# Two reordered stretches of products, one redistributed store tile, and later weight loads in a six-stage perceiver kernel

## The chip, the cores and the metric

The kernel runs on one core of one Trainium2 chip, as one program. The metric is the device time of one execution in microseconds (us), as the median of several runs. The engines are TensorE (PE; its weight loads are listed as PEld), VectorE (DVE), ScalarE (ACT), GpSimd (POOL) and SyncE (SP), which here issues nearly all DMAs.

## What is computed

The reference takes 512 tokens of 256 channels (16 sequences of 32) and a context of 16 x 512 x 256, and adds six sublayers one after the other, each on the layer-normed x:

```python
x = x + _L0_xattn_ref(_layernorm(x), ctx_2048, ...)        # X0: cross-attention, int8 fake-quantised
x = x + _L0_attn_ref(_layernorm(x), ...)                   # A0: differential attention, 16 heads
x = x + _L0_ffn_ref(_layernorm(x), ...)                    # F0: gated feed-forward, fp8 casts
x = x + _L1_xattn_ref(_layernorm(x), ctx_2048, mask, ...)  # X1: masked cross-attention
x = x + _L1_attn_ref(_layernorm(x), ...)                   # M1: latent attention with rope
x = x + _L1_ffn_ref(_layernorm(x), ...)                    # F1: h = square(relu(fp8 matmul)); fp8 matmul
```

In F1 both operands of both products are scaled by their largest absolute value and rounded to fp8 e4m3. For cross-attention the keys and values of all 16 context sequences are projected, and every head's scores run over 512 keys.

## The kernel before

The six stages (X0, A0, F0, X1, M1, F1) are written out as straight code for each engine; semaphores order the engines among each other, and every engine runs its instructions in the order in which they are written. A buffer region in SBUF, the "arena", is divided between the stages, so a weight load of a later stage can only be issued once the earlier owner of its place has finished.

**Units.** Both cross-attentions project context sequence `b` in four units (`unit_pe`, L390 for the keys and L398 for the values; 2 or 4 products each of 128x512 or 128x256; an fp32 product stands as two records in the trace, so these are groups of 4 and 8). Units of X1 already run inside A0 and F0, where PE would otherwise wait: in A0 units 0 to 7, in `attn.pe` (L1241 on).

**X1 by batches.** `batch_cols_pe(b)` runs, for b = 0 to 15: the scores of sequence b (L443, 32 records), the values of sequence b - 1 (`values`, L478: 64 products of 128x32 with 17 columns of weights, 128 records), then up to three units of a later sequence, mixed with the steps that close a row tile (L495, L512, L521). Each group of values raises `x1_pv`, four for a sequence, so `s_pv >= 4 * k` means that the values of the first k sequences are done. DVE clips the scores (L844), evicts some units (L696, L698), and in batches 6 to 13 rounds a piece of F1's weights (`weights_dve`, L1609 and L1402 to L1405).

**Loads beside X1.** SP loads the context of sequence b when unit 4(b - 2) is done (`load_later`), and around it the weights of F1 and M1. For M1 these are five loads for `w_down` and small tables (L1853), three for the rope part of the query weights (L1856, rows of 64 words), two of 768 KB for `wq_upT` (L1861, "heads"), two of 512 KB for `wkv_upT` (L1864, "up"), and two of 1 MB for `wo_rows` (L1868, "out"). PE's first use of the last nine is `fold(0)` (L1897), behind the scores of the last batch and waiting for all nine.

**End of A0.** After the last head's values come the output products of head 14 (`out_rows`, L1232, waiting for ScalarE's copy L1298), unit 3 of X1 (L398), and the transposes of head 15 (L1225).

**End of F1.** The rounded hidden activation is held as a part `high8` (fp8) and a part `low8` (bf16), eight slices h of 128 hidden channels each. 64 products (L1658) add high8[h] and low8[h] times the weights into two PSUM banks: `ACC[0]` for the row tiles t = 0 and 1, `ACC[1]` for t = 2 and 3. A slice's four products, one for each row tile, stand together; high8[h] comes before low8[h - 1]. The last product into a bank raises `s_rows`. Then DVE scales and adds the row tiles of `ORDER` = 0, 1, 3 (L1775), ScalarE scales tile 2 (L1703) and GpSimd adds it to x (L1619); SP stores three tiles (L1788), ScalarE's queue the fourth (L1783). DVE's tile 3 waits for ScalarE's read of the same bank (`s_kept` at 3).

Of the kernel before, what the change touches and what calls it, by code (L numbers as in the profile page):

```python
# [14 lines left out]
P = 128  # L15
NB = 16
SQ = 32
D = 256
NC = D // P
ROWS = NB * SQ  # L20
NT = ROWS // P
# [3 lines left out]
H = 16  # L25
# [72 lines left out]
X0, A0, F0, X1, M1, F1 = range(6)  # L98
# [952 lines left out]
def attn(nc, e, take, sem, d):  # L1051
# [23 lines left out]
    PROJ, TB, ACC = (B[0], B[1]), B[5], (B[6], B[7])  # L1075
# [61 lines left out]
    ORDER, LEAD = (4, 0, 1, 5, 2, 3), 5  # L1137
# [103 lines left out]
    def pe(pe):  # L1241
# [29 lines left out]
        values(pe, H - 1)  # L1271
        out_rows(pe, H - 2)
        for u in units(3):
            e.phases[X1].unit_pe(pe, u)
        turn(pe, H - 1)
        for u in units(4):
# [264 lines left out]
def ffn1(nc, e, take, sem, d):  # L1541
# [22 lines left out]
    BY_ACT, BY_DVE = (2, 4, 6), (0, 1, 3, 5, 7)  # L1564
    ORDER = (0, 1, 3)
    last = wide([P, D])
# [49 lines left out]
    def pool(g):  # L1616
        t = NT - 2
        g.wait_ge(s_kept, 3)
        nc.gpsimd.tensor_tensor(e.X[:, t, :], e.X[:, t, :], last, ALU.add).then_inc(s_last, 1)  # L1619
# [6 lines left out]
    def pe(pe):  # L1626
# [19 lines left out]
        keep_busy(nc, e, HB[1], 10)  # L1646
        for h in range(HT + 1):
            for part, i, first, final in ((high8, h, h == 0, False), (low8, h - 1, False, h == HT)):
                if not 0 <= i < HT:
                    continue  # L1650
                if part is high8:
                    pe.wait_ge(s_h8, 2 * h + 1)
                elif i in BY_ACT:
                    pe.wait_ge(s_relu, HT + BY_ACT.index(i) + 1)
                else:
                    pe.wait_ge(s_y8, 2 + BY_DVE.index(i) + 1)
                for t in range(NT):
                    ins = nc.tensor.matmul(ACC[t // 2][:, (t % 2) * D:(t % 2 + 1) * D], part[:, i, t * P:(t + 1) * P], wp8[:, i, :],  # L1658
                                           start=(first and t % 2 == 0), stop=(final and t % 2 == 1))
                    if final and t % 2:  # L1660
                        ins.then_inc(s_rows, 1)

# [7 lines left out]
    def act(act):  # L1670
# [25 lines left out]
        for h in range(HT):  # L1696
            nc.scalar.activation(z[h], hid[:, h, :], ACT.Square, scale=both[:, 2:3]).then_inc(s_z, 1)
            if h in (4, 6, 7):
                low_act(act, BY_ACT[(4, 6, 7).index(h)])
        t = NT - 2  # L1700
        act.wait_ge(s_rows, 2)
        act.wait_ge(s_scale, 4)
# [21 lines left out]
    def dve(v, done):  # L1724
# [47 lines left out]
        for t in ORDER:  # L1772
            v.wait_ge(s_rows, t // 2 + 1)
            v.wait_ge(s_kept, 3 if t == NT - 1 else 2)
            nc.vector.scalar_tensor_tensor(out=e.X[:, t, :], in0=ACC[t // 2][:, (t % 2) * D:(t % 2 + 1) * D],  # L1775
                                           scalar=both[:, 1:2], in1=e.X[:, t, :], op0=ALU.mult, op1=ALU.add)\
              .then_inc(s_final, 1)
        v.sem_inc(done, 1)

    def store_last(act, out):  # L1780
        t = NT - 2
        act.wait_ge(s_last, 1)
        act.dma_start(out[t * P:(t + 1) * P, :], e.X[:, t, :]).then_inc(e.s_done, 16)  # L1783
# [17 lines left out]
def mla(nc, e, take, sem, d):  # L1801
# [45 lines left out]
    def load(sp):  # L1847
        cols = lambda a: a.rearrange("(c p) n -> p c n", p=P)
        rope_of = lambda i: d.wq_rope_halves[P:QR, :].rearrange("p (j i w) -> p i j w", i=2, w=ROPE)[:, i]
        loads = [(wd, cols(d.w_down)), (scales, d.latent_scales), (cossin, d.rope_rows), (rope, d.rope_cols), (mask32, d.causal)]  # L1850
        assert len(loads) == N_W
        for dst, src in loads:
            sp.dma_start(dst, src, allow_slow_non_contiguous=True).then_inc(s_w, 16)  # L1853
        for dst, src in ((wq0[:, :, 1::2, :], d.wq_rope_halves[0:P, :].rearrange("p (j i w) -> p j i w", i=2, w=ROPE)),
                         (wq1[half(0), :, 1, :], rope_of(0)), (wq1[half(1), :, 1, :], rope_of(1))):
            sp.dma_start(dst, src).then_inc(s_head_in, 16)  # L1856
# [307 lines left out]
    def dve(v, done):  # L2164
# [24 lines left out]
        def residual(t):  # L2189
# [3 lines left out]

    return Named(load_heads=load_heads, load_up=load_up, load_out=load_out, load=load, pool=pool, pe=pe, act=act, dve=dve, during_x1_pe=during_x1_pe, during_x1_act=during_x1_act,
                 during_x1_dve=during_x1_dve, during_x1_pool=during_x1_pool)
# [9 lines left out]
def build(nc, d, out, stages=6):  # L2205
    with ExitStack() as ctx:
# [31 lines left out]
        def _(sp):  # L2238
# [21 lines left out]
            if ph(X1):  # L2260
# [4 lines left out]
                def beside_x1(b):  # L2265
# [4 lines left out]
                    if b == 13 and ph(M1):  # L2270
                        sp.wait_ge(done[F0], 1)
                        sp.wait_ge(phases[X1].s_pv, 4 * 7)
                        phases[M1].load(sp)
                        phases[M1].load_heads(sp, 0)
                    elif b == 14 and ph(M1):
                        phases[M1].load_heads(sp, 1)
                    elif b == 15 and ph(M1):
                        phases[M1].load_up(sp, 0)
                phases[X1].load_later(sp, 3, beside_x1)
                if ph(M1):  # L2280
                    sp.wait_ge(phases[X1].s_pv, 4 * 9)
                    phases[M1].load_up(sp, 1)
                    sp.wait_ge(phases[X1].s_pv, 4 * 10)
                    phases[M1].load_out(sp, 0)
                    sp.wait_ge(phases[X1].s_pv, 4 * 11)
                    phases[M1].load_out(sp, 1)
            if ph(F1):
# [120 lines left out]
```

## Time and profile before

| | us |
|---|---|
| median of 3 runs | 652.62 |
| the runs | 651.98, 652.62, 655.08 |
| the profiled execution | 651.91 |
| its span, first to last instruction | 650.1 |
| PE busy | 634.4 (98%) |
| DVE busy | 417.1 (64%) |
| ScalarE busy | 279.6 (43%) |
| share of PE in the chain that ended last | 89% |

The span is 1.8 us shorter than the time of the same execution. Times of the trace count from the first instruction. The page divides the span in 40 slices of 16.25 us; X1's batches lie between about 390 and 535 us, M1's pairs of heads between 555 and 619, F1 from 620 on. Idle time of an engine is given together with what ended it; "issue" means that nothing which the profile shows held it. Instructions of the engines come by DMA too, in a queue of their own for PE, listed as "instruction".

### The profile page before, as it was taken

How to read it: one execution, taken by the hardware profiler on the slowest of the kernel's cores; microseconds unless marked ns; L12 is line 12 of the kernel's file. 1: busy time of each engine (PE TensorE's matmuls, PEld its weight loads, DVE VectorE, ACT ScalarE, POOL GpSimd, SP SyncE). 2: the span in 40 equal slices, each digit the busy share in tenths (PEclk: the TensorE clock that was granted, in tenths of full speed). 3: DMA queues.
4: the chain of work that ended last, by engine and by line, in shares of the span. 5: the costliest groups of instructions: out<-in, count | busy, mean ns of one | idle time of the engine just before them, and what ended most of it. 6: DMA issues, size and time to landing. Idle time of an engine off the chain costs nothing.

```text
span 650.1 us, 21669 instructions
## 1 busy us (share of the span) xinstructions
PE 634.4 (98%) x9613; PEld 435.0 (67%) x9614; DVE 417.1 (64%) x972; ACT 279.6 (43%) x516; POOL 59.7 (9%) x131
## 2 busy tenths in 40 slices
PE   9999999999999999999999999999979999999997
PEld 5666666667676676666667666777657775456785
DVE  3755467686764665555663772655868965687677
ACT  3454444545353334333343844544435553111156
POOL 1020000000001111101111003000110101000000
PEclk9999999999999999999999999999989999999999
DMA  7242111116006411110013620212373000000001
GB/s 246 66 171 67 35 34 34 68 35 216 15 3 225 134 34 35 34 34 1 2 35 86 208 65 33 68 35 68 80 245 112 24 5 1 2 3 3 4 1 34
DMA packets 28957, 42.25 MB, mean 65 GB/s; under 512 B 6080, under 2 KB 18880, under 8 KB 28352
## 3 DMA queue, kind: packets, MB, share of 16 engines
q1 hardware_dynamic: 28432, 40.47, 19.1%
q8 instruction: 76, 1.25, 0.8%
q10 hardware_dynamic: 432, 0.39, 0.2%
q14 instruction: 17, 0.14, 0.1%
HBM read 40.33 MB, written 0.52 MB: 63 GB/s over the span
## 4 chain that ended last, share of the span: by engine, by line
PE 89%; DVE 8%; issue 2%; ACT 1%; POOLq 0%; DVEq 0%; POOL 0%; ACTq 0%
PE psum L398 17%; PE psum L390 16%; PE psum L1185 7%; PE psum L478 6%; PE psum L443 5%; PE psum L453 4%; PE psum L1161 4%; PE psum L1232 4%; PE psum L1985 2%; PE psum L428 2%; PE psum L1202 2%; PE psum L1962 2%; PE psum L1943 2%; PE psum L1216 1%; DVE arena L2092 1%
## 5 line engine op out<-in xcount | busy, mean ns | idle before, releaser
L398 PE MATMUL psum<-arena 128*128 128x256 f32 x512 | 121.4, 383 | 0.8 <-issue 0.8
L390 PE MATMUL psum<-arena 128*128 128x512 f32 x248 | 118.9, 606 | 0.0
L398 PEld LDWEIGHTS psum<-arena 128*128 128x128 f32 x512 | 94.0, 190 | 22.9 <-issue 10.5
L390 PEld LDWEIGHTS psum<-arena 128*128 128x128 f32 x248 | 44.2, 192 | 41.6 <-issue 40.3
L711 ACT ACTIVATE arena<-arena 128x512 f32<-128x512 f32 x64 | 48.3, 805 | 41.7 <-DVE arena L844 41.7
L1293 ACT ACTIVATE arena<-psum 128x512 f32<-128x512 f32 x48 | 28.4, 597 | 66.2 <-PE psum L1185 37.6
L1185 PE MATMUL psum<-y_cols,arena 128*128 128x512 f32 x112 | 52.1, 599 | 0.0
L705 ACT ACTIVATE arena<-psum,arena 128x512 f32<-128x512 f32 x64 | 40.2, 688 | 27.0 <-DVE arena L831 26.9
L831 DVE TENSOR_REDUCE arena<-psum 128x1 f32<-128x512 f32 x64 | 39.7, 682 | 16.0 <-PE psum L428 15.8
L478 PEld LDWEIGHTS psum<-arena 128*17 128x17 f32 x4096 | 38.6, 96 | 16.0 <-issue 13.6
L685 ACT ACTIVATE arena<-psum,arena 128x512 f32<-128x512 f32 x43 | 29.5, 686 | 45.8 <-PE psum L390 41.1
L844 DVE TENSOR_SCALAR arena<-psum 128x512 f32<-128x512 f32 x64 | 39.7, 681 | 11.8 <-PE psum L443 10.8
L478 PE MATMUL psum<-arena 128*17 128x32 f32 x4096 | 43.1, 197 | 4.0 <-issue 3.9
L687 ACT ACTIVATE arena<-psum 128x512 f32<-128x512 f32 x41 | 24.5, 598 | 47.6 <-PE psum L398 47.5
L1347 DVE TENSOR_REDUCE arena<-psum 128x8 f32<-128x256 f32 x16 | 6.8, 424 | 51.1 <-PE psum L1202 51.1
L443 PEld LDWEIGHTS psum<-arena 64*128 64x128 f32 x512 | 29.8, 188 | 8.0 <-issue 8.0
L328 POOL TENSOR_TENSOR arena<-arena,head_mask 128x64 f32<-128x64 f32 (+1 forms) x64 | 20.7, 348 | 141.7 <-PE psum L428 87.3
L836 DVE COPY arena<-psum 128x512 f32<-128x512 f32 x32 | 22.0, 691 | 17.0 <-PE psum L453 16.5
L443 PE MATMUL psum<-arena 64*128 64x128 f32 x512 | 32.9, 278 | 0.0
L1185 PEld LDWEIGHTS psum<-y_cols,arena 128*128 128x128 f32 x112 | 20.6, 190 | 18.1 <-issue 17.2
L453 PEld LDWEIGHTS psum<-ident,arena 128*128 128x128 f32 x256 | 28.8, 141 | 4.5 <-issue 3.7
L1161 PE MATMUL psum<-arena,y_cols 128*128 128x256 f32 x128 | 31.1, 385 | 0.0
(260 smaller groups left out, 952.6 us busy)
## 6 DMA issues: line engine op xcount, KB each, us to landing
arena<-in_ctxT SPq DMA_DIRECT2D x31, 512.0 KB, 3.7
arena<-in_L_attn_Wv SPq DMA_DIRECT2D x1, 2048.0 KB, 8.1
arena<-in_L_attn_Wq SPq DMA_DIRECT2D x8, 256.0 KB, 2.9
arena<-in_L_attn_Wk SPq DMA_DIRECT2D x8, 256.0 KB, 3.6
arena<-in_L_attn_Wo SPq DMA_DIRECT2D x1, 2048.0 KB, 11.6
arena<-in_L_ffn_w_gating SPq DMA_DIRECT2D x1, 2048.0 KB, 7.8
arena<-in_wo_rows SPq DMA_DIRECT2D x2, 1024.0 KB, 4.9
arena<-in_wq_upT SPq DMA_DIRECT2D x2, 768.0 KB, 7.1
```

What stands on the lines that cost most here:

```text
L390: last = nc.tensor.matmul(bank, wkv[:, c, i * P:(i + 1) * P], x[:, c, :], start=(c == 0), stop=(c == NC - 1))
L398: last = nc.tensor.matmul(bank[:, kk * D:(kk + 1) * D], x[:, c, k * P:(k + 1) * P], wkv[:, c, D:2 * D], start=(c == 0), stop=(c == NC - 1))
L443: ins = nc.tensor.matmul(S[2 * kp + r][:, (2 * kk + h) * P:(2 * kk + h + 1) * P], kT[home(b)][a, h, k * P:(k + 1) * P], qbd[b % QBUFS][a, ...
L453: last = nc.tensor.transpose(S[g][:, k * P:(k + 1) * P], pr[g][:, k * P:(k + 1) * P], e.ident)
L478: last = nc.tensor.matmul(O[b % 2][j * SQ:j * SQ + VW, g * SQ:(g + 1) * SQ], va[home(b)][:, k, head, :], probs[:, j * SQ:(j + 1) * SQ], st ...
L685: ins = nc.scalar.activation(kT[home(b)][:, i, :], U[i % 2], ACT.Identity, bias=bk[:, i:i + 1])
L705: nc.scalar.activation(pr[g], S[g], ACT.Exp, bias=nmx[:, g:g + 1]).then_inc(s_exp, 1)
L711: nc.scalar.activation(pTk[b % 2][k], clip[k // 2][:, k % 2, :], ACT.Exp, bias=mb[:, b, k:k + 1], scale=m01[:, b, k:k + 1]).then_inc(s_exp, 1)
L831: nc.vector.tensor_reduce(nmx[:, g:g + 1], S[g], AX.X, ALU.max, negate=True).then_inc(s_mx, 1)
L844: nc.vector.tensor_scalar(dst, S[i].rearrange("p (a n) -> p a n", n=P), 50.0, -50.0, ALU.min, ALU.max)\
L1161: last = nc.tensor.matmul(bank[:, (t % 2) * 2 * DV:(t % 2 + 1) * 2 * DV], e.yT[:, c, t * P:(t + 1) * P], wv[:, c, p * 2 * DV:(p + 1) * 2 * ...
L1185: last = nc.tensor.matmul(bank, w[:, c, f], e.yT[:, c, :], start=(c == 0), stop=(c == NC - 1))
```

## The change

There are three independent edits.

1. In A0, PE runs unit 3 of X1 before the output products of head 14, no longer behind them.
2. M1's weights are loaded later. The five small loads stay (values of sequence 6 done). The rope loads now wait for the values of sequence 8 and stand between the loads of contexts 14 and 15. The two halves of the heads wait for the values of sequences 9 and 10, the two up loads for those of 11, and the halves of the out weights for those of 12 and 13. Before, rope and heads followed the small loads at once, the first up load came behind context 15, and the second up load and the two out loads waited for sequences 8, 9 and 10.
3. In F1, the last 12 products are written by halves of the row tiles, so that `ACC[0]` is closed by the 8th of them and not by the 10th, and ScalarE and GpSimd finish tile 1 instead of tile 2; DVE's order is 0, 2, 3, and its first tile waits for ScalarE's read.

```diff
         values(pe, H - 1)
-        out_rows(pe, H - 2)
         for u in units(3):
             e.phases[X1].unit_pe(pe, u)
+        out_rows(pe, H - 2)
         turn(pe, H - 1)
...
-    ORDER = (0, 1, 3)
+    ORDER, OTHER = (0, 2, 3), 1
...
-        for h in range(HT + 1):
-            for part, i, first, final in ((high8, h, h == 0, False), (low8, h - 1, False, h == HT)):
...
+        for h in range(HT - 1):
+            pe.wait_ge(s_h8, 2 * h + 1)
+            rows(high8, h, range(NT))
+            if h:
+                low_ready(h - 1)
+                rows(low8, h - 1, range(NT))
+        pe.wait_ge(s_h8, 2 * HT - 1)
+        rows(high8, HT - 1, range(2))
+        low_ready(HT - 2)
+        rows(low8, HT - 2, range(2))
+        rows(high8, HT - 1, range(2, NT))
+        low_ready(HT - 1)
+        rows(low8, HT - 1, range(2))
+        rows(low8, HT - 2, range(2, NT))
+        rows(low8, HT - 1, range(2, NT))
...
-        t = NT - 2
-        act.wait_ge(s_rows, 2)
+        t = OTHER
+        act.wait_ge(s_rows, t // 2 + 1)
...
-            v.wait_ge(s_kept, 3 if t == NT - 1 else 2)
+            v.wait_ge(s_kept, 3 if t // 2 == OTHER // 2 else 2)
...
                         sp.wait_ge(phases[X1].s_pv, 4 * 7)
                         phases[M1].load(sp)
-                        phases[M1].load_heads(sp, 0)
                     elif b == 14 and ph(M1):
-                        phases[M1].load_heads(sp, 1)
+                        sp.wait_ge(phases[X1].s_pv, 4 * 9)
+                        phases[M1].load_rope(sp)
                     elif b == 15 and ph(M1):
-                        phases[M1].load_up(sp, 0)
+                        for k in range(2):
+                            sp.wait_ge(phases[X1].s_pv, 4 * (10 + k))
+                            phases[M1].load_heads(sp, k)
                 phases[X1].load_later(sp, 3, beside_x1)
                 if ph(M1):
-                    sp.wait_ge(phases[X1].s_pv, 4 * 9)
+                    sp.wait_ge(phases[X1].s_pv, 4 * 12)
+                    phases[M1].load_up(sp, 0)
                     phases[M1].load_up(sp, 1)
-                    sp.wait_ge(phases[X1].s_pv, 4 * 10)
-                    phases[M1].load_out(sp, 0)
-                    sp.wait_ge(phases[X1].s_pv, 4 * 11)
-                    phases[M1].load_out(sp, 1)
+                    for k in range(2):
+                        sp.wait_ge(phases[X1].s_pv, 4 * (13 + k))
+                        phases[M1].load_out(sp, k)
```

SP's queue beside X1, from the last M1 table on. In the names, `wq_rope_halves` is the rope part, `wq_upT` the heads, `wkv_upT` up and `wo_rows` out; `x1_pv` is the count of finished values. Before:

```order
L1853 DMA arena<-in_causal 128x256
L1856 DMA arena<-in_wq_rope_halves 128x16x64
L1856 DMA arena<-in_wq_rope_halves 64x8x64 x2
L1861 DMA arena<-in_wq_upT 128x1536
L277 DMA arena<-in_ctxT 128x2x512 [waits x1_unit]
L1861 DMA arena<-in_wq_upT 128x1536
L277 DMA arena<-in_ctxT 128x2x512 [waits x1_unit]
L1864 DMA arena<-in_wkv_upT 128x1024
L1864 DMA arena<-in_wkv_upT 128x1024 [waits x1_pv]
L1868 DMA arena<-in_wo_rows 128x2048 [waits x1_pv] x2
```

The same place in SP's queue after the change:

```order
L1865 DMA arena<-in_causal 128x256
L277 DMA arena<-in_ctxT 128x2x512 [waits x1_unit]
L1871 DMA arena<-in_wq_rope_halves 128x16x64 [waits x1_pv]
L1871 DMA arena<-in_wq_rope_halves 64x8x64 x2
L277 DMA arena<-in_ctxT 128x2x512 [waits x1_unit]
L1876 DMA arena<-in_wq_upT 128x1536 [waits x1_pv] x2
L1879 DMA arena<-in_wkv_upT 128x1024 [waits x1_pv]
L1879 DMA arena<-in_wkv_upT 128x1024
L1883 DMA arena<-in_wo_rows 128x2048 [waits x1_pv] x2
```

Context 14 has moved ahead of the rope loads, and the rope loads, both heads and the first up load have a wait of their own; the number of loads is unchanged.

PE's last products in F1, before (L1658); `f1_high8_low` counts the slices that DVE has written, `f1_relu_low8` and `f1_y8_low8` the low slices of ScalarE and of DVE:

```order
L1658 MATMUL psum<-arena 128x256 [waits f1_high8_low]
L1658 MATMUL psum<-arena 128x256 x3
L1658 MATMUL psum<-arena 128x256 [waits f1_relu_low8]
L1658 MATMUL psum<-arena 128x256 x3
L1658 MATMUL psum<-arena 128x256 [waits f1_y8_low8]
L1658 MATMUL psum<-arena 128x256 x3
```

The same 12 products after the change (L1650):

```order
L1650 MATMUL psum<-arena 128x256 [waits f1_high8_low]
L1650 MATMUL psum<-arena 128x256
L1650 MATMUL psum<-arena 128x256 [waits f1_relu_low8]
L1650 MATMUL psum<-arena 128x256 x3
L1650 MATMUL psum<-arena 128x256 [waits f1_y8_low8]
L1650 MATMUL psum<-arena 128x256 x5
```

The wait for the last low slice stands two products earlier, and four products follow the one that closes the first bank instead of two.

## Rows read from the trace of the kernel before

**Rows 1.** The page: span, and TensorE's granted clock in 40 slices.
```profile
span 650.1 us, 21669 instructions
PEclk9999999999999999999999999999989999999999
```
**Rows 2.** Waits of PE, whole span: who <- for what, us total, times, longest.
```profile
PE psum L478 <- issue: 3.9, 1, 3.9
PE psum L398 <- issue: 0.8, 1, 0.8
PE psum L1232 <- ACT arena L1298: 0.3, 1, 0.3
```
**Rows 3.** PE's timeline in X1: start, us, engine, line, op, tiles, count, [idle before].
```profile
478.39 1.27 PE L478 MATMUL psum<-arena 128*17 128x32 f32 x122
483.51 0.30 PE L478 MATMUL psum<-arena 128*17 128x32 f32 x6 [3.86 <-issue]
483.75 3.31 PE L390 MATMUL psum<-arena 128*128 128x512 f32 x4
...
514.47 1.99 PE L390 MATMUL psum<-arena 128*128 128x512 f32 x4
...
523.63 2.97 PE L398 MATMUL psum<-arena 128*128 128x256 f32 x13 [0.76 <-issue]
...
530.62 0.55 PE L1897 MATMUL psum<-arena 128*128 128x64 f32 x3
```
**Rows 4.** One stretch: busy PE, PEld, DVE, ACT, POOL; clock, DMA share, GB/s.
```profile
483.50:486.50 3.00, 2.99 (x10) 1.36 (x10) 0.00 (x0) 0.00 (x0) 0.00 (x0) 0.51 0.50 145
```
**Rows 5.** DMA queues from 465 to 475 us: packets, MB, share of 16 engines.
```profile
q1 hardware_dynamic: 4089, 2.22, 87.2%
```
**Rows 6.** DMA queues from 475.5 to 476 us, PE's instructions.
```profile
q8 instruction: 1, 0.02, 13.7%
```
**Rows 7.** DMA queues from 476 to 481 us.
```profile
q1 hardware_dynamic: 645, 1.92, 101.2%
```
**Rows 8.** DMA queues from 481 to 481.5 us, PE's instructions.
```profile
q8 instruction: 1, 0.02, 13.5%
```
**Rows 9.** SP's timeline in X1.
```profile
467.32 3.72 SPq L1856 DMA_DIRECT2D arena<-in_wq_rope_halves  x3
...
476.29 0.38 SPq L277 DMA_DIRECT2D arena<-in_ctxT  x1
476.71 7.48 SPq L1864 DMA_DIRECT2D arena<-in_wkv_upT  x2
492.52 8.25 SPq L1868 DMA_DIRECT2D arena<-in_wo_rows  x2
```
**Rows 10.** DMA queues from 520.5 to 521 us, PE's instructions.
```profile
q8 instruction: 1, 0.02, 16.8%
```
**Rows 11.** DMA queues from 504.5 to 505 us, PE's instructions.
```profile
q8 instruction: 1, 0.02, 12.5%
```
**Rows 12.** The loads of line L1868, from issue to landing.
```profile
DMA to landing us min/median/max: 4.9/4.9/4.9
```
**Rows 13.** DVE's timeline at the stop of PE.
```profile
482.15 0.69 DVE L1405 TENSOR_TENSOR arena<-arena 128x512 bf16<-128x512 f32 x1
487.60 0.26 DVE L858 RECIPROCAL arena<-psum 128x16 f32<-128x16 f32 x1 [4.75 <-PE psum L495]
```
**Rows 14.** The chain that ended last, F1's last products: start, us, what.
```profile
639.78 6.43 PE psum L1658 x56
```
**Rows 15.** Timeline of the end.
```profile
646.08 1.27 DVE L1775 SCALAR_TENSOR_TENSOR x_rows<-psum,arena,x_rows 128x256 f32<-128x256 f32 x3 [0.87 <-PE psum L1658]
646.24 0.47 ACT L1703 ACTIVATE arena<-psum,arena 128x256 f32<-128x256 f32 x1 [1.73 <-PE psum L1658]
...
646.85 0.72 POOL L1619 TENSOR_TENSOR x_rows<-x_rows,arena 128x256 f32<-128x256 f32 x1 [23.60 <-ACT arena L1703]
647.61 0.35 ACTq L1783 DMA_DIRECT2D out_x<-x_rows  x1
```

More of the change, by code:

```diff
@@ L1646, in pe, with rows, low_ready @@
         keep_busy(nc, e, HB[1], 10)
-        for h in range(HT + 1):
-            for part, i, first, final in ((high8, h, h == 0, False), (low8, h - 1, False, h == HT)):
[L1649 to L1661, printed above, removed]
+        def rows(part, i, ts):
+            final = part is low8 and i == HT - 1
+            for t in ts:
+                ins = nc.tensor.matmul(ACC[t // 2][:, (t % 2) * D:(t % 2 + 1) * D], part[:, i, t * P:(t + 1) * P], wp8[:, i, :],
+                                       start=(part is high8 and i == 0 and t % 2 == 0), stop=(final and t % 2 == 1))
+                if final and t % 2:
+                    ins.then_inc(s_rows, 1)
+        def low_ready(i):
+            if i in BY_ACT:
+                pe.wait_ge(s_relu, HT + BY_ACT.index(i) + 1)
+            else:
+                pe.wait_ge(s_y8, 2 + BY_DVE.index(i) + 1)
+        for h in range(HT - 1):
[13 more added lines that the diff above has]
+        rows(low8, HT - 1, range(2, NT))
     def keep_x(act, k):
@@ L1699, in act @@
                 low_act(act, BY_ACT[(4, 6, 7).index(h)])
-        t = NT - 2
-        act.wait_ge(s_rows, 2)
+        t = OTHER
+        act.wait_ge(s_rows, t // 2 + 1)
         act.wait_ge(s_scale, 4)
@@ L1780, in store_last @@
     def store_last(act, out):
-        t = NT - 2
+        t = OTHER
         act.wait_ge(s_last, 1)
@@ L1848, in load @@
         cols = lambda a: a.rearrange("(c p) n -> p c n", p=P)
-        rope_of = lambda i: d.wq_rope_halves[P:QR, :].rearrange("p (j i w) -> p i j w", i=2, w=ROPE)[:, i]
         loads = [(wd, cols(d.w_down)), (scales, d.latent_scales), (cossin, d.rope_rows), (rope, d.rope_cols), (mask32, d.causal)]
@@ L1853, in load, with load_rope @@
             sp.dma_start(dst, src, allow_slow_non_contiguous=True).then_inc(s_w, 16)
+    def load_rope(sp):
+        rope_of = lambda i: d.wq_rope_halves[P:QR, :].rearrange("p (j i w) -> p i j w", i=2, w=ROPE)[:, i]
         for dst, src in ((wq0[:, :, 1::2, :], d.wq_rope_halves[0:P, :].rearrange("p (j i w) -> p j i w", i=2, w=ROPE)),
@@ L2192, in dve @@
         finish(nc, v, e, residual, after, done)
-    return Named(load_heads=load_heads, load_up=load_up, load_out=load_out, load=load, pool=pool, pe=pe, act=act, dve=dve, during_x1_pe=during_x1_pe, during_x1_act=during_x1_act,
+    return Named(load_rope=load_rope, load_heads=load_heads, load_up=load_up, load_out=load_out, load=load, pool=pool, pe=pe, act=act, dve=dve, during_x1_pe=during_x1_pe, during_x1_act=during_x1_act,
                  during_x1_dve=during_x1_dve, during_x1_pool=during_x1_pool)
```

## The prediction

> **What bounds the kernel now.** I began with the page. PE is busy in 98% of the span and makes up 89% of the chain that ended last, so only time in which PE stands still or runs slowly, and the tail behind its last product, can be won. Its granted clock is full in all slices but one, the 30th, which begins at 471 us [rows 1]. The view of waits then lists few stops of PE, and the longest is no wait for another engine: 3.9 us of "issue" at L478, the values of X1; behind it come 0.8 us of the same kind at L398 and 0.3 us for ScalarE at the end of A0 [rows 2]. The timeline places the long one. PE stops after 122 of the 128 records of one batch's values, with no semaphore between them, goes on at 483.51, and its next four records of L390 take 3.31 us where the same four take 1.99 us at 514.47 [rows 3]. In those three microseconds the granted clock is 0.51, the 1.2 GHz level: PE had stood still for 3.9 us before [rows 4].
>
> Why does it stop in the middle of a group? The DMA view by short windows gives the reason. PE's own instructions arrive in blocks of 0.02 MB. From 465 to 475 no block arrives at all, only 2.22 MB of data at 87% of the 16 engines [rows 5]. One arrives at 475.5 [rows 6], then again none up to 481 while 1.92 MB of data occupy the engines fully [rows 7], and the next one comes in the half microsecond in which the data end [rows 8]. Its share (13.5% of 8 engine-us) is 1.1 us, so it is in at about 482.3, and PE resumes 1.2 us later. The small stop at L398 is of this kind without any data about: a block that arrives at 520.5 to 521 with 1.3 us [rows 10], and work goes on at 523.63. So PE, which runs through 128 records of values in 1.3 us, empties its store of instructions and, when a block is late, stands. The data are the rope loads from 467.32, heads, contexts 14 and 15 and up, one after the other [rows 9].
>
> Of the Trainium skill, "Runtime: NRT & Kernel Launch" (section "Instruction fetch mechanics") says that instructions are fetched by a DMA queue of the engine's sequencer in blocks of 16 KiB, and that the cost is mostly hidden. The block size agrees with the 0.02 MB; the 3.86 us at 483.51 speak against "hidden" for this stretch. By that rule edit 2 would be worth nothing.
>
> **Edit 1, unit 3 ahead of head 14's output.** Removed: the 0.3 us (0.27 in the timeline) that PE waits for ScalarE's copy [rows 2]. Unit 3 needs only unit 1's eviction, which ScalarE has finished before that copy, and its 1.9 us on PE cover the rest of the copy. The transposes of head 15 stand at the same distance behind both groups, so nothing later moves. **-0.3**, between 0 and -0.3.
>
> **Edit 2, later loads.** What is taken away is the burst between 467 and 481. Up to the end of these values only the small loads and context 14 are left, about 1.3 MB (448, 290 and 512 KB), and they are issued by 468. Nothing is in the engines' way when the block of 475.5 is wanted (earlier, then) and the next one.
> - The stop of 3.86 us. Some of it stays: the block wanted here falls just ahead of a group of values, like that of 520.5, which cost 0.76 us without any data. I take that row for what is left: 3.86 - 0.76 = **-3.1**. Bounds: nothing left (-3.9), or 1.5 us left (-2.4), if the block is one block time of 1.1 us later than in that row.
> - The slow stretch. A stop of 0.76 us at 523 was followed by full clock in every slice of the page. So 3.31 - 1.99 = **-1.3**, with 0 as the other end, if the shorter stop still lowers the clock.
> - Is PE the bound when the stop is gone? During it DVE goes on with its rounding of F1's weights until 482.84, then sits idle for 4.75 us [rows 13]. Without the stop, PE's transposes L495 would be done about 4.6 us before the 487.6 of that row, at 483.0, so DVE, free at 482.84, is just in time. It has no reserve, but it owes nothing either. Cost 0; up to +0.5 if its lag of a few tenths reaches PE.
> - The moved loads. Each costs SP 0.4 to 0.6 us of issue (the three rope loads 3.7 in all [rows 9]), and what is queued behind them on SP is context 15 and the other M1 loads. Context 15 is now behind the values of sequence 8 and the rope loads, at about 484, and PE wants it for unit 60, in batch 13, some 30 us later. All nine loads are wanted at `fold(0)`, 530.62 [rows 3]. The last one is issued after the values of sequence 13, at 521.8 in the old times, and the same load takes 4.9 us to land [rows 12]: 526.7, so 3.9 us are spare. Cost 0.
> - New late blocks. Now a load of 0.75 to 1 MB follows six successive groups of values. The trace has that pattern: the second out load, issued at 500.4 [rows 9], ends at 505.3 [rows 12], and the block of PE in that time arrives at 504.5, at its very end [rows 11]. The waits list no stop of PE for it [rows 2]. So a load does hold a block back, but one load to a batch is about free. The rope loads, with their short pieces, and the two up loads together, are the ones I can't price from such a row. The lower bound is 0. The upper is a block that waits to the end of a 4.9 us load with two such places: half of the 3.86 us, or about +2. I take **+0.5**, near the row at 504.5.
>
> **Edit 3, the last 12 products.** 56 products take 6.43 us, 0.115 us each [rows 14]. `ACC[0]` closes two products earlier, -0.23, and the last product ends when it did. Before, DVE starts on tile 0 at 646.08 and ScalarE at 646.24; GpSimd ends at 647.57 and its tile's store is issued at 647.61, last of all [rows 15]. Now ScalarE can start at about 645.85 and takes 0.47, DVE's first tile waits for it and starts at about 646.36, 0.28 later than before. Its three tiles (1.27 us) end at 647.63, their last store is issued at about 647.75, and GpSimd's branch is 0.4 earlier, at 647.2. The last issue moves from 647.61 to 647.75: **+0.1**, between -0.2 and +0.3. The gain of two products is given back at DVE's new wait.
>
> **The sum.** -0.3 - 3.1 - 1.3 + 0 + 0.5 + 0.1 = -4.1. Against the profiled execution, 651.91 (span 650.1), that is 647.8. The median of the three runs, 652.62, lies 0.7 above the profiled one, so a median after may lie as much above the sum; I say 647.8.
>
> **The rivals.**
> - *The burst goes, a later load costs a stop.* The rope loads at 480.5, or one of the up and out loads between 503 and 518, hold a block until they are through; PE stands about 3.1 us more than undisturbed, and the clock falls for another 1.3. For it: the block of 504.5 came only at the load's end. Against it: that load still cost nothing. -4.1 - 0.5 + 4.4 gives 651.7, no change within the measurement.
> - *The loads are not the cause.* The block would have been late anyway. Against it: in 16 us two blocks came, each when data gave way, and PE stops nowhere else so long. Only edits 1 and 3 count: 651.7. The Trainium skill, "DMA: Bandwidth & Descriptors" (section "SWDGE vs HWDGE vs iDMA"), says that each DMA engine takes its internal queues in turn, by which an instruction block would not have to wait for the data behind which it is queued; the two blocks that arrived at 475.5 and 481 don't look like turns taken.
> - *Slower.* The place is the run of three 1 MB loads behind the values of sequences 11, 12 and 13, where the block of 520.5 already costs 0.76 us with no data about. If two of these loads and the rope loads each cost what the burst cost beyond that, 3.1 + 1.3, it is 13.2 lost against 4.6 won: 660. It decides from 4.6 us lost in total, that is from the second such stop.
> - *The edit's clock part fails.* The stop shrinks but the slow stretch stays: 649.1. This is inside the forecast's own range.
>
> **How the numbers follow.** Forecast (a block's residue of 0 to 1.5 us, later stops up to 2 in all, clock regained): 0.70, with its own range 646.2 to 649.8. A later load costs one full stop: 0.14. Loads not the cause: 0.06. Slower: 0.07. Something between forecast and first rival, 649.8 to 651: 0.03. The predicted time is that of the forecast. To leave out no more than 2 in 10, the range has to reach over the first two rivals, to 652.0; below, 646.0 is the forecast with nothing left of the stop and no new cost (651.9 - 0.3 - 3.9 - 1.3 - 0.2 = 646.2). A measurement of this kernel can tell a difference of about 0.5%, 3.3 us: faster is below 649.4. The forecast's range lies there but for its end, and gives 0.69; the two rivals near 651.7 and that end give 0.23; slower 0.08.
>
> **What would show it.** Right: no idle of PE over 1 us at L478 in X1, the 30th slice of the clock at full, L390 behind it at about 2.0 us for four records, blocks of instructions arriving every 4 to 8 us between 464 and 481, `fold(0)` without a wait, and at the end DVE's first tile starting behind ScalarE's read. Wrong: a stop of 1 us or more in a later batch with a load's end beside it (first rival, or the slower one if there are several), or a stop at the same records with the DMA engines empty (second rival). DVE's eviction L696 or its clipping L844 named as what PE waits for would show that DVE has become the bound.

## The result and the profile after

The changed kernel takes 647.11 us (median of 5 runs, 646.73 to 647.78), beside 655.05 us for the kernel before in the same runs (651.98 to 655.63): ratio 0.9896, 95% interval 0.9869 to 0.9923. On another chip, later, it was 647.47 us and 0.9916 (0.9900 to 0.9931). So it is 0.8 to 1.0% faster, more than the 0.5% that can be told apart here. The forecast, 647.8 us, lies 0.7 above the first median. The kernel before varies from one execution to the next by 3 us or more, the changed one by 1 to 2. Two executions of the runs below, of 717 and of 2160 us, are far from all others and are left out.

The profiled execution took 646.73 us, 5.2 less than that of before. The page's header and the clock, against [rows 1]:

```profile
span 644.9 us, 21670 instructions
...
PEclk9999999999999999999999999999999999999999
```

The slow slice is gone. PE's waits for "issue" now stand far down the list, at 0.8 and 0.4 us where [rows 2] has 3.9 and 0.8:

```profile
PE psum L478 <- issue: 0.8, 2, 0.6
...
PE psum L398 <- issue: 0.4, 1, 0.4
```

PE's timeline over the same places as [rows 3] (start, us, engine, line, tiles, count, idle before):

```profile
478.07 1.27 PE L478 MATMUL psum<-arena 128*17 128x32 f32 x122
479.89 0.24 PE L478 MATMUL psum<-arena 128*17 128x32 f32 x6 [0.55 <-issue]
480.06 1.99 PE L390 MATMUL psum<-arena 128*128 128x512 f32 x4
...
518.04 2.97 PE L398 MATMUL psum<-arena 128*128 128x256 f32 x13 [0.39 <-issue]
...
525.03 0.66 PE L1912 MATMUL psum<-arena 128*128 128x64 f32 x4
```

The stop still stands behind the 122nd record, but is 0.55 us long and not 3.86; the four records of L390 take 1.99 us and not 3.31; `fold(0)` starts at 525.03 and not at 530.62, 5.6 us earlier, with no wait for its weights. What SP does now, against [rows 9]:

```profile
467.39 0.43 SPq L277 DMA_DIRECT2D arena<-in_ctxT  x1
480.17 3.41 SPq L1871 DMA_DIRECT2D arena<-in_wq_rope_halves  x3
483.63 0.62 SPq L277 DMA_DIRECT2D arena<-in_ctxT  x1
487.51 8.25 SPq L1876 DMA_DIRECT2D arena<-in_wq_upT  x2
502.30 1.89 SPq L1879 DMA_DIRECT2D arena<-in_wkv_upT  x2
509.40 7.64 SPq L1883 DMA_DIRECT2D arena<-in_wo_rows  x2
```

Between 468 and 480 SP issues no load, and the data of context 14 are in by 471.2; after that nothing comes until 480 but instructions. In the DMA view, the block that had come at 481 to 481.5 [rows 8] comes in the window from 477 to 478, and the one before it, which had come at 475.5 [rows 6], in the window from 472 to 473. The two windows of the changed kernel:

```profile
q8 instruction: 1, 0.02, 6.0%
...
q8 instruction: 1, 0.02, 8.8%
```

The windows from 464 to 481, first before, then after (PE, PEld, DVE, ACT, POOL busy, granted clock, DMA share, GB/s):

```profile
464.00:481.00 17.00, 15.66 (x349) 12.20 (x349) 15.99 (x33) 8.53 (x15) 2.76 (x7) 1.00 0.87 267
```
```profile
464.00:481.00 17.00, 16.45 (x356) 12.52 (x355) 16.00 (x33) 8.22 (x14) 2.75 (x7) 1.00 0.29 79
```

DVE is as busy in both; what differs is the DMA share and PE's idle time (1.3 us and 0.6). The end of the kernel, against [rows 15]:

```profile
640.42 0.49 PE L1650 MATMUL psum<-arena 128*128 128x256 bf16 x3
...
640.51 0.47 ACT L1716 ACTIVATE arena<-psum,arena 128x256 f32<-128x256 f32 x1 [1.30 <-PE psum L1650]
641.12 1.27 DVE L1788 SCALAR_TENSOR_TENSOR x_rows<-psum,arena,x_rows 128x256 f32<-128x256 f32 x3 [1.20 <-ACT arena L1716]
641.12 0.72 POOL L1619 TENSOR_TENSOR x_rows<-x_rows,arena 128x256 f32<-128x256 f32 x1 [23.16 <-ACT arena L1716]
641.88 0.35 ACTq L1796 DMA_DIRECT2D out_x<-x_rows  x1
```

The last product ends at 640.91, and the span ends 4.0 us behind that; before it was 3.9 (646.2 and 650.1).

### The profile page after: what moved, and what is told of

It reads as the page before. It is cut to its first block, busy times and chain, and to the rows that moved or that the text cites. A ratio compares the mean times of both kernels' runs of the same rounds, so it can differ in the third digit from the quotient of the medians.

```text
span 644.9 us, 21670 instructions
## 1 busy us (share of the span) xinstructions
PE 632.7 (98%) x9614; PEld 434.5 (67%) x9614; DVE 417.3 (65%) x972; ACT 279.8 (43%) x516; POOL 59.6 (9%) x131
## 4 chain that ended last, share of the span: by engine, by line
PE 89%; DVE 8%; issue 1%; ACT 1%; DVEq 0%; POOL 0%; ACTq 0%; POOLq 0%
PE psum L398 17%; PE psum L390 16%; PE psum L1185 7%; PE psum L478 6%; PE psum L443 5%; PE psum L453 4%; PE psum L1161 4%; PE psum L1232 4%; PE psum L2000 2%; PE psum L428 2%; PE psum L1202 2%; PE psum L1977 2%; PE psum L1958 2%; PE psum L1216 1%; DVE arena L2107 1%
## 5 line engine op out<-in xcount | busy, mean ns | idle before, releaser
L398 PE MATMUL psum<-arena 128*128 128x256 f32 x512 | 121.5, 383 | 0.4 <-issue 0.4
L390 PE MATMUL psum<-arena 128*128 128x512 f32 x248 | 117.5, 600 | 0.0
L398 PEld LDWEIGHTS psum<-arena 128*128 128x128 f32 x512 | 93.9, 190 | 22.6 <-issue 10.3
L390 PEld LDWEIGHTS psum<-arena 128*128 128x128 f32 x248 | 43.7, 190 | 41.1 <-issue 39.8
L478 PEld LDWEIGHTS psum<-arena 128*17 128x17 f32 x4096 | 38.5, 96 | 12.9 <-issue 10.6
L478 PE MATMUL psum<-arena 128*17 128x32 f32 x4096 | 42.9, 196 | 0.9 <-issue 0.8
```

Source lines behind the costliest of these rows:

```text
L390: last = nc.tensor.matmul(bank, wkv[:, c, i * P:(i + 1) * P], x[:, c, :], start=(c == 0), stop=(c == NC - 1))
L398: last = nc.tensor.matmul(bank[:, kk * D:(kk + 1) * D], x[:, c, k * P:(k + 1) * P], wkv[:, c, D:2 * D], start=(c == 0), stop=(c == NC - 1))
L478: last = nc.tensor.matmul(O[b % 2][j * SQ:j * SQ + VW, g * SQ:(g + 1) * SQ], va[home(b)][:, k, head, :], probs[:, j * SQ:(j + 1) * SQ], st ...
```

## The experiments

Each kernel was compared with the kernel before on the same chip. Ratios are to it, with the 95% interval. "Block" is a 16 KB block of PE's instructions. The main theory, A, is that of the prediction: blocks come late while the DMA engines are full of data.

### Where in the change is the gain?

**The kernel before, once more** (`e0_before_again`), with no edit.

> The kernel before once more, unchanged, for a second trace. Its timed runs lay at 652 and at 655 us, those of the changed kernel within 1.1 us. Theory A (blocks of PE's instructions wait for the data that are queued ahead of them): the slow stretch near 480 us is the part that varies between executions, so a time of about 655 goes with a stop of PE at L478 of 6 to 7 us instead of 3.9, or a second stop beside it, and all other stages agree with the first trace within 0.5 us. Rival B (the executions differ everywhere, by the clock or by memory): the 3 us are spread over the stages or lie in a clock dip elsewhere, and the stop at L478 is 3.9 us as in the first trace.

Measured: 653.34 us (651.84 to 655.70, 10 runs), ratio 1.0011 (0.9993 to 1.0029). The profiled execution, 652.82 us, has the stop at the same record, a little shorter (3.06 us), and four small ones of 0.2 to 0.7 us elsewhere, of which the longest is shown:

```profile
PE psum L478 <- issue: 3.3, 2, 3.1
PE psum L521 <- issue: 0.7, 1, 0.7
```

No execution near 655 us was caught with a profile, so which stage makes it is open, and neither A nor B is decided for the variation. Two things are seen. The stop is not a constant (3.1 us here, 3.9 in the first trace). And the granted clock, which is on record for every execution, says more than the traces. One slow stretch of 3.4 us, as in both traces, gives a mean of 0.997; 6.8 us at the lower level, as in the longer burst below, give 0.995. Of 81 executions of this kernel, 41 have a mean of 0.996 to 0.997 (median 653.2 us), 27 one of 0.993 to 0.995 (654.0), and 13 have 0.999 or 1.000 (651.3). So by this estimate the slow stretch comes once in half of the executions, about twice in a third, and not at all in a few. With all loads moved and no tiny products, the mean is 0.999 or 1.000 in all 21 executions counted below. The clock is not all of it: without a slow stretch the kernel before still takes 3 to 4 us more than these.

**Only the later loads** (`e1_loads_only`), the second edit on the kernel before. Its diff is the SP part of the one shown for the change.

> Only the second edit, the later loads, on the kernel before. Theory A: all but 0.3 us of the gain is here. The stop at L478 falls from 3.9 to about 0.55 us, the four records of L390 behind it take 2.0 us, and the time is 647.0 to 647.6, within 0.4 us of the whole change. Rival C (part of the gain comes from the products' order in the first or last edit): the time stays 1 us or more above that of the whole change.

Measured: 648.30 us, ratio 0.9926 (0.9913 to 0.9938). The stop, in the timeline:

```profile
480.96 0.24 PE L478 MATMUL psum<-arena 128*17 128x32 f32 x6 [0.28 <-issue]
481.14 1.99 PE L390 MATMUL psum<-arena 128*128 128x512 f32 x4
```

**The first and the third edit without the loads** (`e2_without_loads`):

> The first and the third edit without the later loads. Theory A: the stop of 3.9 us and the slow stretch stay, the first edit gives 0.3 us and the third costs 0.1 to 0.3, so the time equals that of the kernel before within 0.4 us. Rival C: it is 1 us or more below it.

Measured: 652.87 us, ratio 0.9994 (0.9980 to 1.0009).

```profile
483.26 0.30 PE L478 MATMUL psum<-arena 128*17 128x32 f32 x6 [3.34 <-issue]
483.50 3.47 PE L390 MATMUL psum<-arena 128*128 128x512 f32 x4
```

Theory A holds here by the second run: the loads alone give 0.74%, the other two edits nothing that can be measured, and the intervals of the loads alone and of the whole change overlap. The first run alone would not have decided it. Its time was 0.7 us above the top of what I had written down, and it lies 1.2 us above the first median of the whole change (where rival C began, at 1 us) and 0.8 above the second, each from a comparison of its own.

### What in the burst holds the block?

**A longer burst** (`e3_longer_burst`):

```diff
                     phases[M1].load_up(sp, 0)
             phases[X1].load_later(sp, 3, beside_x1)
             if ph(M1):
-                sp.wait_ge(phases[X1].s_pv, 4 * 9)
                 phases[M1].load_up(sp, 1)
-                sp.wait_ge(phases[X1].s_pv, 4 * 10)
                 phases[M1].load_out(sp, 0)
-                sp.wait_ge(phases[X1].s_pv, 4 * 11)
                 phases[M1].load_out(sp, 1)
```

> The kernel before, with the second up load and both out loads issued at once behind the first up load: 2.5 MB more in the burst, at 0.38 MB/us 6.5 us more, so that the data end near 488 instead of 481. Theory A (a block waits until what is queued ahead of it has gone through): the block of PE's instructions arrives near 488, the stop at L478 is 9 to 11 us, the clock falls for longer, and the time is 6 to 9 us above the kernel before. Rival D (the DMA engines take turns between the queues, the stop has another cause): the block arrives at 481 as before, the stop is 3.5 to 4.5 us and the time unchanged.

Measured: 656.20 us, ratio 1.0049 (1.0030 to 1.0069), so 3.2 us slower; neither theory's number. The stop is 5 us. In the DMA view the block comes between 483 and 484, in the middle of the data: 1.74 MB more follow until 489 (first window 483 to 484, then 484 to 489).

```profile
485.99 0.30 PE L478 MATMUL psum<-arena 128*17 128x32 f32 x6 [4.98 <-issue]
486.22 3.78 PE L390 MATMUL psum<-arena 128*128 128x512 f32 x4
```
```profile
q1 hardware_dynamic: 75, 0.41, 103.3%
q8 instruction: 1, 0.02, 6.6%
...
q1 hardware_dynamic: 244, 1.74, 83.6%
```

So my strong form of A, that a block waits until all data are through, falls. Longer data do make the block later (the stop grew by 1.1 us against the first trace, and the clock stayed low for about twice as long), but the last data of the burst don't hold it. These are the two out loads, issued at 478.9 and 479.4; when PE's block was asked for can't be seen, so whether it passed data that stood ahead of it, or only data behind it, is open. What is left is a weaker form: while the engines are full, a block takes some microseconds more.

**Half of the loads moved.** First, the rope loads stay with the small ones (`e4_rope_early`); heads, up and out go where the change has them (the end of the diff is as in the change), and context 15 no longer waits for the values of sequence 8:

```diff
                         phases[M1].load(sp)
-                        phases[M1].load_heads(sp, 0)
-                    elif b == 14 and ph(M1):
-                        phases[M1].load_heads(sp, 1)
+                        phases[M1].load_rope(sp)
                     elif b == 15 and ph(M1):
-                        phases[M1].load_up(sp, 0)
+                        for k in range(2):
+                            sp.wait_ge(phases[X1].s_pv, 4 * (10 + k))
+                            phases[M1].load_heads(sp, k)
...
```

> The later loads on the kernel before, but with the three rope loads left where they were, behind the small loads: of the burst, small loads, rope and context 14 stay together (2.05 MB, most of its short packets), heads, context 15 and up are moved. After the longer burst, theory A reads: a block of PE's instructions that is asked for while the DMA engines are full takes 4 to 5 us instead of 1, whatever comes behind. The block wanted near 477 is asked for when these data are through, so PE's stop at L478 is 0.3 to 0.8 us and the time 647.5 to 649, as with all loads moved. Rival E (the many short packets of the rope loads are what blocks): the stop stays over 2.5 us and the time over 651.

Measured: 650.15 us, ratio 0.9968 (0.9944 to 0.9992). The stop is 2.0 us, between the two theories, at full clock in this execution. It was the fastest of seven, 649.04 us with a mean clock of 0.999; five of the others have 0.997, so they most likely had a longer stop and a slow stretch.

```profile
482.06 0.25 PE L478 MATMUL psum<-arena 128*17 128x32 f32 x6 [2.00 <-issue]
482.24 1.99 PE L390 MATMUL psum<-arena 128*128 128x512 f32 x4
```

I had overlooked context 15. In this kernel it moves 0.47 MB between 476 and 479.5, when the block is due, and the block comes in the next half microsecond (windows 476 to 479.5 and 479.5 to 480):

```profile
q1 hardware_dynamic: 232, 0.47, 44.6%
...
q8 instruction: 1, 0.02, 12.1%
```

The stop is 1.5 us longer than in the changed kernel, but this run doesn't show that one 512 KB load costs all of that. The rope loads are early too, and the block before comes late with them: at 474.9, where the changed kernel has 472.4 (1.8 us later, counted from the start of the group of values). The shortest spacing of two blocks hereabouts is 3.7 us, so the next one could have come at 478.6; it came at 479.8. By this estimate context 15 costs up to 1.2 us and the block before the rest; no run has context 15 early alone. It is a part of the change that its diff hardly shows: the rope loads' new wait stands ahead of context 15.

**Only the rope loads later** (`e5_rope_late`): all else in the burst stays.

```diff
                         phases[M1].load(sp)
                         phases[M1].load_heads(sp, 0)
...
                     sp.wait_ge(phases[X1].s_pv, 4 * 9)
+                    phases[M1].load_rope(sp)
                     phases[M1].load_up(sp, 1)
```

> The other half: only the three rope loads are moved, behind the values of sequence 8; heads, contexts 14 and 15 and the first up load stay. Theory A: context 15 and up (1 MB, issued near 476.5) still fill the engines when the block wanted near 477 is asked for, so the stop is 2 to 3.5 us, with the slow stretch behind it if it is over 3, and the time 650 to 652. Rival E (short packets): the stop is under 1 us and the time 647.5 to 649.

Measured: 652.58 us, ratio 0.9983 (0.9972 to 0.9994).

```profile
485.11 0.25 PE L478 MATMUL psum<-arena 128*17 128x32 f32 x6 [3.65 <-issue]
```

The stop is whole with the rope loads gone, so their many short packets are not what blocks: rival E falls. The stop and the time are just above the ranges that A had (3.5 us and 652). This trace also has a stop of 1.4 us at 195.14, in X0, with the DMA engines idle (share 0.00 from 193 to 196), where the kernel before, with the same program on PE, has none. So single executions differ by a stop of this size for a reason that no run here shows.

**Only context 15 and the first up load later** (`e11_only_the_last_two`):

```diff
                         phases[M1].load_heads(sp, 1)
+                        sp.wait_ge(phases[X1].s_pv, 4 * 9)
```

> One line on the kernel before: SP waits for the values of sequence 8 between the second half of the heads and context 15. So small loads, rope, heads and context 14 (3.6 MB) keep their places, and only context 15 and the first up load, 1 MB of the 4.7, come some 4 us later. Theory A in the form that the runs with one half of the loads moved leave (only data in flight when PE's block is asked for, near 477 to 479, matter): the 3.6 MB are through by 478 to 479, the block arrives before 480, the stop at L478 is 0.4 to 1.7 us and without a slow stretch, and the time 648 to 650. Rival F (it is the sum of the burst, since the block before, wanted near 471.5, is late too and pushes the next one back): the stop stays 2.5 to 4 us and the time over 651.

Measured: 649.46 us, ratio 0.9952 (0.9933 to 0.9970).

```profile
482.28 0.25 PE L478 MATMUL psum<-arena 128*17 128x32 f32 x6 [1.97 <-issue]
482.45 1.99 PE L390 MATMUL psum<-arena 128*128 128x512 f32 x4
```

One line gives more than half of the gain: the loads in flight when the block is due. The rest, a stop of 2.0 us against 0.28 to 0.57 in the five traces with all loads moved, goes with the 3.6 MB before it. They make the previous block late (it arrives at 476.2), and the next one comes 3.8 us behind it, about the shortest spacing seen here, although the data have nearly ended by 478.5. In the kernel before the two come 5.6 us apart, and these 1.8 us are about what the stop is longer by (3.86 against 1.97). So both theories have a part: what is in flight, and the block before.

### Is it the block, or the place?

**Borders shifted by half a block** (`e6_shifted_blocks`), on the kernel before:

```diff
+    for _ in range(32):
+        nc.tensor.matmul(bank[0:17, 0:32], e.neghalf[:, 0:1].to_broadcast([P, 17]), e.neghalf[:, 0:1].to_broadcast([P, 32]),
+                         start=True, stop=True)
...
-            first_busy(nc, e, e.B[5], 2)
+            first_busy(nc, e, e.B[5], 1)
```

> The kernel before with its loads unchanged; only 32 tiny products (17 columns of weights, 32 wide) are added at the very start, behind the first of the two filler products there, the second of which is left out. They lengthen PE's program by about 128 instructions, half a block, and every border between blocks falls half a block earlier in the program. Theory A: the stop goes where the border goes. PE would run dry near 478.9, after about 50 of the 128 records of that group and not 122, and maybe a first time near 472.3 in the group before; the block for 478.9 is asked for about 4 us earlier than before, so the stops come to 0 to 2.5 us together and the time falls by 1.5 to 4.5 us. Rival B (the place is special for another reason: a hazard, the memory, the values' own reads): the stop is again behind the 122nd record, 3 to 4 us, and the time within 1 us of the kernel before.

Measured: 656.36 us, ratio 1.0049 (1.0031 to 1.0067), slower where I had expected faster. But the place is decided. The long stop in X1 is gone, with the loads of X1 unchanged; a stop of the same size stands in X0, at 163, where PE never stopped before, with the slow clock behind it (clock 0.71):

```profile
163.44 0.29 PE L478 MATMUL psum<-arena 128*17 128x32 f32 x11 [3.03 <-issue]
...
163.50:166.50 3.00, 3.00 (x21) 2.38 (x21) 0.00 (x0) 0.33 (x2) 0.00 (x0) 0.71 0.49 156
...
485.00:490.00 5.00, 5.00 (x167) 4.06 (x166) 4.70 (x9) 2.75 (x5) 0.00 (x0) 1.00 1.04 378
```

From 485 to 490 the burst fills the DMA engines (share 1.04), and PE is busy all the time. At 163 it is another burst, A0's first weights (the windows from 155 to 160.5 and on to 161):

```profile
q1 hardware_dynamic: 1829, 1.94, 102.9%
...
q8 instruction: 1, 0.02, 13.8%
```

In the kernel before, these weights are loaded in the same way (share 1.09 from 160 to 162, with a block in the middle of them), and PE doesn't stop. Rival B falls. What I hadn't counted is the price elsewhere: PE's stops at L478 come to 8.1 us in seven places, and the tiny products themselves, 2.75 us for a filler product of about 1.9, held PE up by 1.1 us at the start.

**A quarter of a block, on the changed kernel** (`e10_after_quarter_shift`), 16 tiny products in place of 32.

> The changed kernel with 16 tiny products at the start (and the second filler product left out), so that the borders of PE's instruction blocks fall a quarter of a block earlier. Theory A: the two stops that are left, 0.55 us near 480 and 0.4 to 0.9 us near 518, go, since the border is past the group of values; others may come where a border now falls just before such a group or into the loads of another stage (as in the run shifted by half a block, whose 3.0 us came at 163). Taken over all of it the time is 646 to 649. Rival B (the two stops belong to their places): they stay where they are.

Measured: 650.60 us, ratio 0.9966 (0.9950 to 0.9981), so 3 us worse than the changed kernel and 1.6 above the top of what I expected. The two small stops near 480 and 518 are gone, others have come, among them these:

```profile
47.63 0.29 PE L478 MATMUL psum<-arena 128*17 128x32 f32 x11 [1.06 <-issue]
...
119.47 0.29 PE L478 MATMUL psum<-arena 128*17 128x32 f32 x10 [1.21 <-issue]
```

So the small stops go with the borders too (one trace, and e5 shows that one of 1.4 us can come without a change in PE's program). Of the two positions tried on the changed kernel, and of the two tried on the kernel before, the one without tiny products is the better.

### The changed kernel again, and its end

**Once more** (`e7_after_again`), unedited:

> The changed kernel once more, on the chip and beside the runs of the kernel before of this call. Theory A: 646.7 to 648, ratio 0.990 to 0.993, stops of 0.3 to 0.8 us at L478 near 480 and at L398 near 518, full clock throughout. Rival C (a chip on which the kernel before was slow made the first ratio of 0.9896): the ratio is over 0.994.

Measured: 647.47 us, ratio 0.9916 (0.9900 to 0.9931). PE's stops:

```profile
PE psum L398 <- issue: 0.9, 1, 0.9
PE psum L478 <- issue: 0.8, 2, 0.6
```

The gain doesn't hang on the chip of the first comparison.

**The old row tiles with the new order of products** (`e8_old_tiles`), and **tile 0 last** (`e9_tile0_last`), each on the changed kernel:

```diff
-    ORDER, OTHER = (0, 2, 3), 1
+    ORDER, OTHER = (0, 1, 3), 2
...
-            v.wait_ge(s_kept, 3 if t // 2 == OTHER // 2 else 2)
+            v.wait_ge(s_kept, 3 if t == NT - 1 else 2)
```
```diff
-    ORDER, OTHER = (0, 2, 3), 1
+    ORDER, OTHER = (2, 3, 0), 1
```

> The changed kernel, with the products still by halves but the old division of the row tiles: DVE takes 0, 1, 3 and ScalarE and GpSimd tile 2. Count from the start of the last product. With the changed kernel the first bank is read by ScalarE 0.12 us before it and DVE starts 0.49 us behind it, the last of DVE's three tiles ends 1.75 us behind it, and the span ends 4.27 us behind it (kernel before: 4.16). If what the new order won is lost only in DVE's wait for ScalarE, then DVE starts here 0.1 us before the last product, and ScalarE and GpSimd are the last ones again as in the kernel before: the end comes 4.1 to 4.2 us behind the last product, 0.1 less than with the changed kernel. If the tail is set by the stores alone, it stays at 4.2 to 4.35.

> The changed kernel with DVE's tiles in the order 2, 3, 0, so that its first tile waits for the second bank and no longer for ScalarE's read. The second bank closes 0.27 us behind the start of the last product, so DVE can start at 0.3 to 0.4 us instead of 0.49: the end moves by -0.1 to -0.2 us, if DVE's chain is what ends last, and not at all if it isn't.

Measured: 647.39 us, 0.9909 (0.9889 to 0.9930), and 647.88 us, 0.9914 (0.9894 to 0.9933): no difference between these and the changed kernel can be told by the times. By the traces, the span ends 3.94 us behind the start of the last product with the old tiles and 4.19 with tile 0 last, 0.1 less than the changed kernel, as expected; the changed kernel has 4.27 in both its traces. This distance hardly varies: it is 4.14 to 4.16 in all eight traces with the old end of F1, and 4.27 in all four with the new one. With the old tiles (last product's end 641.79):

```profile
641.46 1.43 DVE L1788 SCALAR_TENSOR_TENSOR x_rows<-psum,arena,x_rows 128x256 f32<-128x256 f32 x3 [0.65 <-PE psum L1650]
641.83 0.47 ACT L1716 ACTIVATE arena<-psum,arena 128x256 f32<-128x256 f32 x1 [1.73 <-PE psum L1650]
```

DVE starts ahead of the last product's end, as expected, and the end is 0.3 us earlier than with the new tiles, more than the 0.1 that I expected. Part of it is how long the last stores take to land, which one trace for each can't settle. So, by one trace, the products by halves are worth 0.2 us with the old tiles (3.94 against 4.15), and the new division gives that back.

## Why the prediction was right

- **The cause.** The prediction took the stop at L478 for a late block of instructions and the data for its reason. Both hold: the stop goes with the block's border (shifted borders) and with the data in flight (loads alone, halves of the loads). What was too simple is that a block comes when the data give way. That was a misreading of its own rows: the block of 475.5 came while the engines were full on both sides, as [rows 7] shows from 476 on. In the longer burst a block came with 1.74 MB still to follow, and the run with only the last two loads moved shows that the block before matters too.
- **The size of the gain.** The sum was taken from the profiled execution, 651.91 us, a fast one. The kernel before has medians of 652.7 to 655.05 in the five comparisons, and between medians the whole change gains 7.9 us in the first comparison and 5.9 in the second; between the profiled executions it is 5.2. The forecast had 4.1 from that execution, 4.8 from the median of three. That the time came within 0.7 us is in part luck: what the slower executions of the kernel before have on top is gone with the change too, and nothing in the prediction says why.
- **What is left of the stop.** Taken as 0.76 from the stop at 523.63, measured 0.55 (0.3 to 0.6 in the other traces with all loads moved): -3.3 and not -3.1.
- **The slow stretch.** -1.3, measured 3.31 - 1.99 = -1.3. The short stop doesn't lower the clock.
- **DVE just in time.** DVE ends its weights at 482.53 and starts L858 at 482.59, PE's L495 ends at 482.49; nobody waits. As worked out.
- **New late blocks.** Taken as +0.5. The stop at L398 was 0.39 in this trace (0.76 before), and 0.8 to 1.0 in the four others with all loads moved: about 0, between -0.4 and +0.2. This is the term that was mis-sized, on the safe side; none of the later loads met a block that was due at a bad moment.
- **Context 15.** I took its new wait for a cost of 0 and no gain. By the run with the rope loads early, its move is worth up to 1.2 us, an estimate; in the sum it was hidden in the stop.
- **The first edit.** -0.3: head 15's transposes start at 344.21, not 344.54.
- **The end.** +0.1, measured 4.27 against 4.16 from the start of the last product to the end of the span. DVE's wait for ScalarE is where the gain of two products goes.

The sum of the trace is -5.2 and the forecast was -4.1; of the 1.1 us between, about 0.9 is the term for new late blocks and 0.2 the stop. "The loads are not the cause" and "slower" are out. "A later load costs a full stop" didn't happen here; the kernel with its borders shifted by half a block shows that a burst elsewhere can cost one (3.0 us at 163) when a border meets it.

On the two pages of the Trainium skill: the blocks of "Runtime: NRT & Kernel Launch" (section "Instruction fetch mechanics") are seen here, and so is, for most of them, that their cost is hidden: 76 come in the trace of before, and three stops of 0.2 us or more stand in it. The one of 3.86 us is the exception. The turns between queues in "DMA: Bandwidth & Descriptors" (section "SWDGE vs HWDGE vs iDMA") fit the longer burst, where a block came with 1.74 MB of data still to go, better than my strong form did. A turn was not short, though: counted from the start of the group of values, the block came 4.6 us later than in the changed kernel, with no data about.

## What to carry to other kernels

A wait of PE for "issue" in the middle of a group, with no semaphore there, is worth a look at the DMA view in windows of half a microsecond: if an instruction block arrives just before PE goes on, move the loads that are in flight then, even one of 512 KB, and spread the loading of weights over the time up to their first use. Short products run through instructions fastest (122 records in 1.27 us here), and nearly all of the stops of 1 us or more stood in such groups. Whoever adds or removes instructions shifts all later borders, and can lose 3 us in a stage that the edit never touched, as here at 163; compare the "issue" waits of the whole trace before crediting an edit.

## What the runs showed of the hardware

- A block of PE's instructions takes about 1.1 us to come (0.9 to 1.7 in these traces), and PE went on 1.2 to 1.6 us behind the end of the one for which it stood near 480. Counted from the start of the group of values, the two blocks around 472 to 478 came 2.6 to 3.7 us earlier with idle DMA engines (changed kernel) than with full ones (the kernel before, both traces).
- Two blocks were never closer than about 3.7 us in these stretches (3.3 anywhere in the traces). So one that is late can make the next one late, as in e11: 476.2, then 479.9.
- PE's clock fell to the 1.2 GHz level behind stops of 3.0, 3.1, 3.3, 3.65, 3.9 and 5.0 us, and not behind those of 2.0 us or less (e4 and e11 among them). Behind those near 480 the fall cost PE 1.3 us or more (four records of L390 in 3.3 to 3.8 us where 2.0 is usual).
